# Transposed slab loads issued inside the normalisation scan, and two PSUM copies moved from ScalarE to VectorE

## The reference

```python
x = x + attn_a(layernorm(x))     # no softmax, so it is linear in the scores; rotary part
x = x + ffn(layernorm(x))        # silu(x @ gate.T * gs) * (x @ up.T * us), then @ down.T * ds; 5632 wide
x = x + attn_b(layernorm(x))     # 16 heads, 4 key/value heads, causal softmax, 128 per head
x = x + ffn(layernorm(x))        # the same weights again
# layernorm: (x - mean) / sqrt(var + 1e-5), no scale or shift
# attn_b: scores = q @ k.T; masked; softmax; @ v; @ Wo.T + bo
```

## Time and profile before

| what | us |
| --- | --- |
| median of 5 runs | 18078.2 |
| lowest and highest of the 5 runs | 17012.96 and 18446.47 |
| the profiled execution, its time | 17012.96 |
| the profiled execution, its span on the slowest core (core 1) | 17011.4 |
| spans of the 8 cores | 16875.3 to 17011.4 |
| PE busy on that core | 13136.8 (77%) |
| DVE, ACT, POOL busy | 2920.8, 2738.2, 625.3 |

### The profile page before, as it was taken

The page is one execution under the profiler, slowest core; times in us unless marked ns, Lnnn a source line. Parts: engine busy times, 40 slices in busy tenths (PEclk is TensorE's granted clock), DMA queues, the critical chain, the costliest instruction groups (busy, mean ns, idle before and its releaser), DMA issues.

```text
span 17011.4 us, 156451 instructions; the slowest of 8 cores (16875.3 to 17011.4 us)
## 1 busy us (share of the span) xinstructions
PE 13136.8 (77%) x55442; PEld 5255.8 (31%) x55442; DVE 2920.8 (17%) x4638; ACT 2738.2 (16%) x4006; POOL 625.3 (4%) x1000
## 2 busy tenths in 40 slices
PE   0566656738998999995686777888865999999989
PEld 0222322313443444442331111221212444444444
DVE  1212223331111111112113222111122111111111
ACT  1100010010000000001102344446541000000000
POOL 0000000010000000000000000000000000000000
PEclk9977868869999999997897888888887999999999
DMA  8688864454444444454561111110124444444443
GB/s 139 164 155 156 158 125 113 122 166 153 155 169 157 158 147 158 151 169 165 192 171 51 46 45 44 44 44 10 38 88 176 158 158 149 152 152 171 158 158 144
DMA packets 667023, 2223.44 MB, mean 131 GB/s; under 512 B 388793, under 2 KB 415650, under 8 KB 546858
## 3 DMA queue, kind: packets, MB, share of 16 engines
q1 hardware_dynamic: 245194, 1781.27, 30.9%
q0 software_dynamic: 72928, 348.19, 9.5%
q10 hardware_dynamic: 348160, 83.97, 3.5%
HBM read 2024.45 MB, written 348.13 MB: 139 GB/s over the span
## 4 chain that ended last, share of the span: by engine, by line
PE 67%; DMA 17%; DVE 5%; another core or an unknown queue 4%; issue 3%; ACT 2%; ACTq 2%; SPq 0%; DVEq 0%; POOL 0%; POOLq 0%
PE ps L500 28%; PE pm L537 13%; PE ps L847 10%; PE ps L586 7%; PE pm L847 5%; DMA lnh<-lnt 5%; DMA ws<-wr_ffn_down_w 4%; DVE smf L915 3%; PE pm L958 2%; ACTq L146 2%; DMA ws<-wr_attn_b_Wo 1%; PE ps L958 1%; ACT lnt L965 1%; ACT lnt L441 1%
## 5 line engine op out<-in xcount | busy, mean ns | idle before, releaser
L500 PE MATMUL ps<-lnf,ws 128*128 128x512 bf16 x22528 | 4899.7, 381 | 205.3 <-DMA ws<-wr_ffn_gate_w 145.1
L500 PEld LDWEIGHTS ps<-lnf,ws 128*128 128x128 bf16 x22528 | 2210.0, 98 | 2897.2 <-issue 265.0
L537 PE MATMUL pm<-ws,big 128*128 128x512 bf16 x11264 | 2572.7, 393 | 480.2 <-DMA ws<-wr_ffn_down_w 413.4
L537 PEld LDWEIGHTS pm<-ws,big 128*128 128x128 bf16 x11264 | 1127.0, 101 | 1925.9 <-issue 689.7
L510 ACT ACTIVATE med<-ps,gs 128x512 bf16<-128x512 f32 x704 | 483.8, 687 | 7228.8 <-PE ps L500 7228.8
L515 DVE SCALAR_TENSOR_TENSOR big<-ps,us,med 128x512 bf16<-128x512 f32 x704 | 528.7, 751 | 4438.5 <-PE ps L500 4438.5
L586 PE MATMUL ps<-lnf,ws 128*128 128x512 bf16 x3072 | 703.3, 393 | 583.5 <-DMA lnf<-lnh 449.7
L965 ACT ACTIVATE lnt<-pm,cm 128x512 bf16<-128x512 f32 x1536 | 1045.0, 688 | 536.6 <-PE pm L958 523.0
L847 PE MATMUL ps<-lnt,c_ones_col 128*1 128x512 bf16 x2304 | 960.3, 417 | 97.0 <-ACT lnt L965 93.1
L847 PE MATMUL pm<-lnt,big 128*128 128x512 bf16 x2304 | 989.9, 430 | 0.0
L847 PE MATMUL ps<-lnf,ws 128*128 128x512 bf16 x2560 | 569.2, 385 | 344.5 <-DMA lnf<-lnh 306.4
(11 more groups left out here) (100 smaller groups left out, 5664.6 us busy)
## 6 DMA issues: line engine op xcount, KB each, us to landing
ws<-wr_ffn_gate_w SPq DMA_DIRECT2D x176, 2048.0 KB, 7.8
ws<-wr_ffn_up_w SPq DMA_DIRECT2D x176, 2048.0 KB, 9.9
ws<-wr_ffn_down_w SPq DMA_DIRECT2D x256, 1408.0 KB, 8.2
lnh<-lnt POOLq DMA_DIRECT2D x256, 256.0 KB, 5.2
res_a<-smf POOLq DMA_DIRECT2D x256, 256.0 KB, 4.4
xt<-res_a SPq DMA_DIRECT2D x64, 1024.0 KB, 5.7
smf<-res_a SPq DMA_DIRECT2D x256, 256.0 KB, 6.5
ws<-wr_attn_b_Wq SPq DMA_DIRECT2D x32, 2048.0 KB, 10.6
```

Of the source, the lines that this page charges most:

```text
L500: ici=ici: t.matmul(pbuf.h[:, :], wbuf.h[:, hc * 512 + ici * 128: hc * 512 + (ici + 1) * 128], lnf.h[:, hc * 512:(hc + 1) * 512], start=(h ...
L537: icl=icl, tsub=tsub, first=first, last=last: t.matmul(po.h[:, :], hb.h[:, hci * 512 + tsub * 128: hci * 512 + (tsub + 1) * 128], wd.h[:, ...
```

## The change

`emit_ln_scan` takes a hook, which it calls after every fourth row tile, that is when a slab is complete. The three sublayer functions give it a hook that issues `load_lnf` for slab 0 and slab 1 (into the two `lnf` buffers) at that place, and remembers it; the loop over the slabs then leaves these two loads out. The second loop of attention A is as before. In attention B, the copies at L924 and L981 are made by DVE (`tensor_copy`) and no longer by ACT (`copy`), at the same places in the order of the program.

```diff
-    def emit_ln_scan(SRC):
+    def emit_ln_scan(SRC, hook=None):
...
+            if i % 4 == 3 and hook is not None:
+                hook(sl)
...
+    def lnf_prefetch_hook(pre):
+        def hook(sl):
+            if sl < 2:
+                load_lnf(LNF[sl % 2], sl)
+                pre.add(sl)
+        return hook
...
     def emit_ffn(SRC, DST, dst_h):
         drain_conv()
-        emit_ln_scan(SRC)
+        pre = set()
+        emit_ln_scan(SRC, lnf_prefetch_hook(pre))
...
             lnf = LNF[s % 2]
-            load_lnf(lnf, s)
+            if s not in pre:
+                load_lnf(lnf, s)
...
-            mk.op("a", lambda a, pzb=pzb, zr=zr: a.copy(
+            mk.op("v", lambda v, pzb=pzb, zr=zr: v.tensor_copy(
                 zr.h[:, :], pzb.h[:, :]), reads=[pzb], writes_acc=[zr])
...
-                mk.op("a", lambda a, pout=pout, h=h: a.copy(
+                mk.op("v", lambda v, pout=pout, h=h: v.tensor_copy(
                     aout.h[:, h * 512:(h + 1) * 512], pout.h[:, :]),
                     reads=[pout], writes=[aout])
```

## The result

The changed kernel took 18049.8 us (median; 17508.2 to 18443.2), the kernel before in the same comparison 18138.0 (16969.1 to 18497.3). The ratio on record, of the quickest executions of each, is 1.049, 95% interval 1.036 to 1.062. It can't be read as the cost of the change: in most executions of either kernel some cores run part of the time at a third clock level, and no execution of the change in this comparison is free of it. Its quickest, 17508 us, with a mean clock of 0.85 on one die, stands beside 16969 and 17013 us of before, which is 1.03 times and not 1.049, so the ratio moves by per cents with the executions that are taken; the second of the two is the profiled execution of before and has no third level.

What follows compares the result with a forecast made beforehand. PE waits bound it: idle before attention B's broadcast and row-sum matmuls, and latency-chained normalisation scans through ACT. Terms +62 - 108 = -46 took 17013.0 to 16967 us; own range 16880 to 17060, upper end on record 18150.

Steps and rivals of the forecast that it cites:

- Part 1: Slabs 0 and 1 loaded inside the normalisation scans: 172 us added less 110 saved, a cost of 62 us (2 to 194).
- A hold: In each scan after tiles 3 and 7, 16 transpose issues keep ACT's queue and delay the scan 21.5 us each time.
- the starts': At the four sublayers' starts the first matmul waits only for its first weights: 31 + 25 + 29 + 25 = 110 us saved.
- free hold: Rival, chance 0.08: ACT idles in the scan anyway, so issues cost only 8 x 2 = 16 us; time 16811 us.
- backed-up hold: Rival, chance 0.15: each load takes 38 us in the scan, as at the FFN's start; time 17099 us.
- Part 2: Both attention B copies moved from ACT to DVE: 74 + 59 - 25 = 108 us gained (49 to 167).
- the clock's term: In attention B's long heads, the clock rises sooner once the idle is filled: 59 us, between 0 and 118.
- the block's end: At the end of each block of 16 heads the output projection starts 3.1 us later: 8 x 3.1 = 25 us lost.
- I take half: Of the 2.4 us between long and short heads, 49 times, half was counted as gained: 59 of 118 us.
- the early clock: Rival, chance 0.12: all 49 long heads in attention B become short, another 59 us gained; time 16908 us.
- The idle: PE's 0.61 us wait before the row-sum matmul at head boundaries goes: 60 us in blocks 1 to 7, 74 together.
- 0.04 to each side: Chance given to the whole kernel's time changing by 2% (340 us) either way, with 0.92 for no change.

Runs made afterwards that it cites:

- the first experiment: The changed kernel run again, unaltered, beside the kernel before: median 17827 us (17379 to 18529) against 17770 us.
- with zeros: Normalised rows written as zeros in the changed kernel and the kernel before: 16857 to 16894 us against 16926 to 16992, ratio of means 0.9947.
- the spread hook: Against the changed kernel, two transposes after each of tiles 9 to 24 instead of 16 after tiles 3 and 7: median 17628 us (17503 to 18318).
- the early reciprocal: Against the kernel with both copies on DVE, reciprocal and narrowing put right behind the result's copy: median 17123 us (16558 to 17902).

## Why the prediction was right or wrong

**Part 1, right.** A hold of 22.0 us (30.5 less the 8.5 of the earlier trace rows) stood against 21.5, the scans' +179 against 172, the starts' -116 against 110. Its sum of +62 is +48 to +63 in the runs. The free hold and the backed-up hold are both out. The Trainium skill (DMA: Bandwidth & Descriptors, "Issuing engines are not separate DMA queues") calls the sequencer's time to start a DMA usually small beside the DMA itself; here an issue took 1.31 us (20.96 us for 16), where a transpose of this trace lands 4.4 us after its issue (median), so it does not agree.

**Part 2, the mechanism right, the clock's term too small.** Of the three terms, the block's end was right: 25 forecast, 3.16 us each and 25 in all measured (from the last matmul of the last head to the output projection, medians over all cores of the first experiment, 13.56 us for 10.40). Head 14's broadcast comes 1.7 us later, and the two broadcasts are 5.40 us apart instead of 4.06, since DVE copies head 14's before it takes head 15's reciprocal (timeline, core 4, end of block 6, beside the earlier trace rows):

```profile
11765.26 0.69 DVE L996 CAST lnf<-pm 128x512 bf16<-128x512 f32 x1 [1.02 <-PE pm L861]
11765.87 3.33 DVE L930 RECIPROCAL smf<-ps 1x512 f32<-1x512 f32 x1
...
11770.55 0.69 DVE L939 COPY smf<-ps 128x512 f32<-128x512 f32 x1 [0.83 <-PE ps L935]
11771.16 3.33 DVE L930 RECIPROCAL smf<-ps 1x512 f32<-1x512 f32 x1
...
11778.26 5.96 PE L861 MATMUL ps<-ws,lnf 128*128 128x512 bf16 x16 [2.41 <-POOL lnf L941]
```

The heads then gained 147 + 25 = 172 where I had 74 + 59 = 133. The step that failed is "I take half". The intervals between broadcasts in block 6 (medians over the cores without the third level) were 31.16 and 33.48 us and are all 30.73 now, apart from the last of a block. So the whole difference between the kinds went, 49 x 2.32 = 114, nearly the early clock's 118, the rival that I gave 0.12. The idle, on the other hand, was over-sized: a short head became 0.43 us shorter and not 0.61, which is 42 of the 60 us for blocks 1 to 7. Nothing in the earlier trace rows spoke for a half; I split the difference between two bounds. The two copies tried singly show that the same idle made all the long heads: it goes with the result's copy, and they with it. The Trainium skill (TensorE: Matmul & The Clock Gate, "A second HAM failure mode: psum-queue depth-cycling") puts such a clock down to short idles between groups of matmuls; the trace agrees, with one kind of head at 0.89 where the idle is gone.

**The sum.** -46 was forecast, -91 (30 either way) measured with zeros, -101 in the stretches (-84 in those that the change touches). From the 17013.0 of the profiled execution that is some 16920, inside my own range of 16880 to 17060, between the forecast and the early clock.

**The clock of the two kernels, the step that failed for the number on record.** The forecast took the clock to be the same for both kernels but for the heads; a third level had no term in the sum, and no reason was given for leaving it at nothing. No case of mine made the kernel slower by 2%, and no run shows that the change does. But I read the five times of before, 17013 to 18446 for one program, as something that "one profile" can't explain, moved the upper end for it, and still gave 0.04 to each side, as if both kernels would be met at the same clock. They were not. What was on record as 4.9% slower is 61 us a slab wherever a core is at 0.8125, 6807 us of core 2 in the profiled execution of after, against none in that of before. The missing rival was a third clock level; that the shown times spread over 8% was the row that spoke for it. The Trainium skill (TensorE: Matmul & The Clock Gate, "Seeing it yourself") describes such a level, 13/16, for a whole die from its third busy core on, and says that zero operands don't bring it; the runs agree on the level and on the zeros, and, read as in the last section, on the die. I had weighed no such rule.

**Open.** How much of the third level an execution has goes by how long the two pairs of cores of a die run at the same time (last section). What sets that is open. Dies without it were 12 of 66 for before in the three sets of runs, 6 of 44 for the change in the two, 7 of 14 with the hook alone, 6 of 16 with either copy alone, 2 of 12 with both, none of 16 with the spread hook, 2 of 12 with slab 0 from SyncE, 4 of 12 with the early reciprocal and 2 of 14 with slab 0 from ScalarE added. These counts show no order by density, and they can't tell a small difference: they count mainly how the pairs happened to start.

## What to carry to other kernels

Where the same program's times spread by 8%, look for the clock before trusting a ratio: compare stretch by stretch over cores at the same level, or with operands that keep the level away. Ask also whether the cores really run at the same time: here executions of one program differed by 8%, and by the traces what differed was how long the cores of a die ran together. A DMA issue is work of the queue that issues it: 16 in a row held a chain of latencies for 21 us, one to a tile cost nearly nothing. And the wait worth removing stood in the first profile: 573 us ahead of the broadcast, plus the half-speed stretch behind each; moving its producer up in DVE's order took 652 us off the version with both copies, where the whole change took off some 100.

## What the runs showed of the hardware

```profile
10582.00:10620.00 38.00, 34.02 (x124) 12.36 (x122) 4.82 (x7) 0.00 (x0) 3.78 (x7) 0.81 0.61 194
10649.50:10655.50 6.00, 5.89 (x22) 1.35 (x21) 0.56 (x2) 4.79 (x8) 0.00 (x0) 1.00 0.00 1
```

```profile
16311.80:16349.80 38.00, 37.74 (x144) 15.70 (x146) 3.75 (x5) 2.90 (x5) 0.00 (x0) 0.81 0.29 111
16379.30:16385.30 6.00, 5.95 (x28) 2.74 (x28) 0.46 (x1) 0.69 (x1) 0.00 (x0) 1.00 0.00 0
```

The cores are at different work there, yet they change together. As I read it, cores 2 and 3 had started 5.7 ms before cores 0 and 1, and the level lasts from the first dense work of the later pair to the end of the earlier one's run. All 17 dies that show the level in the ten traces that have it are of this form, each with one shift between its pairs, from 3.1 to 15.0 ms. The later pair meets it 540 to 727 us into its run, as its dense work begins; it ends within the last 0.4 ms of the earlier pair's run, except on three dies where the later pair keeps it for another 0.1 to 0.7 ms. Outside the overlap two dies have it once, for 5 us, on one pair. In the overlap it pauses while one pair has no dense work: core 2 shows none from 9504 to 9796, when, by the shift, core 0 is in its second scan. This is read from the coincidence of the changes; no record gives the starts themselves. It fits the Trainium skill (TensorE: Matmul & The Clock Gate, "Seeing it yourself"), which has the whole die fall. It also says how before's profiled execution can be dense on all eight cores and have none of the level: its pairs need not have run at the same time. The time of an execution then grows with the overlap: the changed kernel's pairs shared 11.5 ms on one die and 10.5 on the other in the profiled execution of after (17869.9 us), and 4.4 ms on one die alone in the first experiment's (17379 us).

ScalarE's queue issues transposes while ScalarE computes (2.46 us of issue from 3665.51, an activation from 3665.50). The square root behind both starts at 3668.08, 0.1 us after the issue's end, but VectorE had released it only then too, so that row does not show a hold; the 27.14 us of "issue" ahead of the square root in the profiled execution of after do.
